# Token variance of a metaformer block: from VectorE to GpSimd, between two gate products, with new first and last steps

## What is computed

```python
x = x + attention(ln_c(x))            # windows of 8x8, 4 heads of 16, relative bias, projection
t = tokens(x)                         # 64 channels a token
n = (t - mean(t)) / sqrt(var(t) + 1e-5)
p = softmax(n @ router_w + router_b)  # 8 experts, the best two, their weights made to sum to 1
t = t + sum over the two of p_e * (n @ expert_w[e] + expert_b[e])
```

## Time and profile before

| | us |
|---|---|
| median of 3 runs | 1184.91 |
| lowest, highest | 1181.35, 1187.77 |
| the profiled execution | 1189.28 |
| its span, first to last instruction | 1187.5 |
| PE busy | 1053.8 (89%) |
| DVE busy | 891.9 (75%) |
| ACT busy | 745.1 (63%) |
| POOL busy | 429.3 (36%) |

### The profile page before, as it was taken

One profiled execution on the slowest core, in us unless ns is written; L12 is line 12 of the kernel. 1 busy time (PEld: TensorE's weight loads), 2 busy tenths in 40 slices (PEclk: granted clock), 3 DMA queues, 4 the chain that ended last, 5 costly groups with the idle time before them and its releaser, 6 DMA issues.

```text
span 1187.5 us, 39116 instructions
## 1 busy us (share of the span) xinstructions
PE 1053.8 (89%) x16838; PEld 602.3 (51%) x16838; DVE 891.9 (75%) x1441; ACT 745.1 (63%) x1217; POOL 429.3 (36%) x423
## 2 busy tenths in 40 slices
PE   5987899999899989999998988999998989988754
PEld 3654455555455555555555554555555545554311
DVE  4667777898787778988877776888887877678652
ACT  2777566766676677776676664767766666655400
POOL 1004244334424433344334333334442343335543
PEclk9999899999999999999999998999999999998877
DMA  5016476788776667887876667777776778647787
GB/s 183 2 38 155 98 162 165 177 187 192 185 165 162 162 169 172 186 196 182 198 166 142 160 160 170 180 173 175 178 175 152 182 179 198 140 100 170 189 182 176
DMA packets 49255, 192.48 MB, mean 162 GB/s; under 512 B 10558, under 2 KB 10814, under 8 KB 32572
## 3 DMA queue, kind: packets, MB, share of 16 engines
q1 hardware_dynamic: 49084, 189.98, 67.3%
HBM read 154.04 MB, written 18.87 MB: 146 GB/s over the span
## 4 chain that ended last, share of the span: by engine, by line
PE 77%; DMA 7%; issue 7%; DVE 5%; POOL 2%; ACT 1%; SPq 0%; POOLq 0%; ACTq 0%; DVEq 0%
PE bank L654 16%; PE bank L549 11%; PE bank L566 11%; PE bank L540 6%; PE bank L583 6%; DMA gz<-gates_dram 5%; PE bank L527 5%; PE bank L590 5%; PE bank L497 4%; PE bank L602 3%; PE bank L611 2%; PE bank L629 2%; PE bank L640 2%; PE bank L488 1%; PE bank L474 1%
## 5 line engine op out<-in xcount | busy, mean ns | idle before, releaser
L1480 POOL TENSOR_TENSOR gz<-gz,tt 128x1024 f32<-128x1024 f32 x96 | 240.5, 2506 | 134.0 <-DMA gz<-gates_dram 134.0
L654 PE MATMUL bank<-gz,wex 64*64 64x512 f32 x2048 | 262.1, 617 | 22.6 <-DVE gz L1682 17.2
L1076 ACT ACTIVATE pt<-bank 128x512 f32<-128x512 f32 x256 | 151.6, 592 | 140.2 <-PE bank L566 139.9
L1667 DVE TENSOR_TENSOR probs<-bank,mx 128x1024 f32<-128x1024 f32 x128 | 156.7, 1224 | 98.4 <-PE bank L566 95.3
L1682 DVE TENSOR_TENSOR gz<-gz,tt 128x1024 f32<-128x1024 f32 x160 | 201.4, 1277 | 26.4 <-DMA gz<-gates_dram 26.4
L1452 POOL TENSOR_TENSOR tt<-prj,xs 128x512 f32<-128x512 f32 x64 | 80.4, 1278 | 318.3 <-ACT prj L1093 318.3
L1660 DVE TENSOR_REDUCE mx<-bank 128x16 f32<-128x1024 f32 x128 | 156.1, 1220 | 36.0 <-PE bank L549 34.9
L566 PE MATMUL bank<-cst,probs 128*128 128x128 f32 x1024 | 167.6, 287 | 2.4 <-ACT pt L1076 1.6
L549 PE MATMUL bank<-km,qs 32*64 32x128 f32 x4096 | 146.8, 278 | 16.0 <-issue 16.0
L566 PEld LDWEIGHTS bank<-cst,probs 128*128 128x128 f32 x1024 | 113.1, 143 | 85.4 <-issue 72.0
L549 PEld LDWEIGHTS bank<-km,qs 32*64 32x64 f32 x4096 | 113.5, 133 | 65.1 <-issue 65.1
(11 more groups left out here) (110 smaller groups left out, 1429.2 us busy)
## 6 DMA issues: line engine op xcount, KB each, us to landing
gz<-gates_dram SPq DMA_DIRECT2D x256, 512.0 KB, 10.3
xs<-in_x SPq DMA_DIRECT2D x32, 512.0 KB, 9.0
tx<-tt SPq DMA_DIRECT2D x128, 128.0 KB, 2.9
out<-ob SPq DMA_DIRECT2D x128, 128.0 KB, 10.1
gz<-in_rel SPq DMA_DIRECT2D x1, 2048.0 KB, 8.1
gates_dram<-gt_rs SPq DMA_DIRECT2D x32, 64.0 KB
cst<-in_consts SPq DMA_DIRECT2D x1, 359.0 KB, 2.9
tt<-in_weights SPq DMA_DIRECT2D x4, 64.0 KB, 8.9
```

The lines of the kernel that those rows point to most:

```text
L654: last = mm(bank[64 * x:64 * x + 64, Y_BANK + a, :], wex[64 * a:64 * a + 64, e, :], gz[64 * a:64 * a + 64, s.pair(e)[1], e % 2, x * CH:(x ...
L1076: af(pt[g % 2][:, u % 2, :, :, :, :].rearrange("p j h x q -> p (j h x q)"), bank[:, PT_BANK, :], ACT.Copy).then_inc(pt_ready, 1)
L1480: tt_(gz[:, k, e % 2, :], gz[:, k, e % 2, :], tt[s.buf(4)][:, :], op=ALU.mult).then_inc(z_pool, 1)
L1667: tt_(probs[g % 2][:, :, :, :].rearrange("p h w (m k) -> p (h w m) k", k=N), two_banks(S_BANK).rearrange("p (c k) -> p c k", k=N), mx[g % ...
```

## The change

The three operations of token_statistics go from VectorE to GpSimd, with a semaphore of their own, moment. In the loop they stand between GpSimd's gated(c-6, 7) and gated(c-5, 1). VectorE's chain through top has two steps less. The warm-up and the drain have new orders on all five queues. The loop's orders on the other engines stay. The core of the diff; of the reordered lists only parts are shown:

```diff
+        moment = sem("moment")
-        TOP = 16
+        TOP = 14
...
 @@ SyncE, warm-up
             load_weights()
+            load_relative()
             load(strips[0])
             move_selection()
-            load_relative()
...
 @@ SyncE, drain
             spread_gates(strips[-5], 0)
             spread_gates(strips[-5], 1)
+            store(strips[-7])
+            swap_tokens(strips[-5])
             spread_gates(strips[-5], 2)
             spread_gates(strips[-5], 3)
...
+            write_gates(strips[-2])
             store(strips[-4])
-            swap_tokens(strips[-2])
-            write_gates(strips[-2])
             spread_gates(strips[-2], 0)
...
             write_gates(strips[-1])
-            store(strips[-3])
+            swap_tokens(strips[-2])
             spread_gates(strips[-1], 0)
             spread_gates(strips[-1], 1)
             spread_gates(strips[-1], 2)
             spread_gates(strips[-1], 3)
+            store(strips[-3])
...
 @@ GpSimd
+            def token_statistics(s):
+                pool.wait_ge(L_ready, s.count(2, 2))
+                wait(pool, lnr_done, s.count(1, 0))
+                tt_(mq[:, :, :, :], st_[:, :, 0:2, :], st_[:, :, 0:2, :], op=ALU.mult).then_inc(moment, 1)
+                pool.wait_ge(moment, s.count(2, 1))
+                tt_(vr[:, :].rearrange("p (c t a) -> p t c a", c=2, a=2), st_[:, :, 2:4, :], mq[:, :, :, :],
+                    op=ALU.subtract).then_inc(moment, 1)
+                pool.wait_ge(moment, s.count(2, 2))
+                nc.gpsimd.tensor_scalar(vr[:, :], vr[:, :], 0.0, 1e-5, ALU.max, ALU.add).then_inc(stat_ready, 1)
...
 @@ GpSimd, loop
                 gated(strips[c - 6], 7)
+                token_statistics(strips[c - 4])
                 gated(strips[c - 5], 1)
                 place_gates(strips[c - 4])
...
 @@ GpSimd, drain
             gated(strips[-5], 7)
+            place_gates(strips[-4])
             residual(strips[-3], 0)
             residual(strips[-3], 1)
-            place_gates(strips[-4])
...
             gated(strips[-3], 1)
-            gated(strips[-3], 4)
-            gated(strips[-3], 7)
             place_gates(strips[-2])
             residual(strips[-1], 0)
             residual(strips[-1], 1)
+            gated(strips[-3], 4)
+            gated(strips[-3], 7)
+            token_statistics(strips[-1])
             gated(strips[-2], 1)
             place_gates(strips[-1])
...
 @@ VectorE
-            def token_statistics(s):
-                dve.wait_ge(L_ready, s.count(2, 2))
-                top_step(s, 1, tt_(mq[:, :, :, :], st_[:, :, 0:2, :], st_[:, :, 0:2, :], op=ALU.mult))
-                top_step(s, 2, tt_(vr[:, :].rearrange("p (c t a) -> p t c a", c=2, a=2), st_[:, :, 2:4, :],
-                                   mq[:, :, :, :], op=ALU.subtract))
-                nc.vector.tensor_scalar(vr[:, :], vr[:, :], 0.0, 1e-5, ALU.max, ALU.add).then_inc(stat_ready, 1)
...
 @@ VectorE, warm-up
+            one_hot()
             norm_ready()
             variance(strips[0])
             guard_variance(strips[0])
             split_std(strips[0])
             scale_x(strips[0])
-            one_hot()
...
 @@ VectorE, loop
                 move_logits(strips[c - 4])
-                token_statistics(strips[c - 4])
                 normalise(strips[c - 3], 0)
                 gated(strips[c - 5], 0)
```

More of the change, by code:

```diff
@@ L398, in _ @@
             spread_gates(strips[-4], 2)
+            swap_tokens(strips[-4])
             spread_gates(strips[-4], 3)
             write_gates(strips[-3])
+            store(strips[-5])
             spread_gates(strips[-3], 0)
@@ L661, in _ @@
             channel_sums(strips[0])
+            bias_rows()
             spread_std(strips[0])
@@ L892, in _ @@
             denominators(strips[-3], 3)
-            transposes(strips[-2], 1)
+            transposes(strips[-2], 0)
+            experts(strips[-6], 4)
             experts(strips[-6], 5)
@@ L1132, in _ @@
             square_mean(strips[0])
+            square(strips[1])
             log_var(strips[0])
@@ L1138, in _ @@
             move_k(strips[0], 1)
-            square(strips[1])
             square_mean(strips[1])
@@ L1490, in _ @@
             residual(strips[1], 1)
+            token_statistics(strips[1])
             gated(strips[0], 1)
+            gated(strips[0], 4)
             place_gates(strips[1])
-            gated(strips[0], 4)
             residual(strips[2], 0)
@@ L1798, in _ @@
             shift(strips[1], 0)
+            scale_x(strips[2])
             normalise(strips[0], 2)
@@ L1802, in _ @@
             normalise(strips[0], 3)
-            scale_x(strips[2])
             row_max(strips[1], 2)
             shift(strips[1], 2)
-            normalise(strips[1], 0)
             row_max(strips[1], 3)
@@ L1817, in _ @@
             top_two(strips[0])
+            normalise(strips[1], 1)
             pick_two(strips[0])
+            split_std(strips[3])
+            gates(strips[0])
+            row_max(strips[2], 0)
             normalise(strips[1], 2)
-            row_max(strips[2], 0)
             shift(strips[2], 0)
-            gates(strips[0])
+            scale_x(strips[3])
             normalise(strips[1], 3)
@@ L1825, in _ @@
             shift(strips[2], 1)
-            split_std(strips[3])
             row_max(strips[2], 2)
             shift(strips[2], 2)
-            scale_x(strips[3])
             row_max(strips[2], 3)
-            normalise(strips[2], 0)
-            shift(strips[2], 3)
             variance(strips[4])
@@ L1835, in _ @@
             move_logits(strips[1])
-            token_statistics(strips[1])
+            shift(strips[2], 3)
+            normalise(strips[2], 0)
             logits(strips[1])
@@ L1842, in _ @@
             split_std(strips[4])
+            gated(strips[0], 0)
             gates(strips[1])
@@ L1955, in _ @@
             normalise(strips[-2], 0)
+            row_max(strips[-1], 0)
+            shift(strips[-1], 0)
             move_logits(strips[-3])
-            token_statistics(strips[-3])
+            gated(strips[-4], 0)
+            normalise(strips[-2], 1)
+            row_max(strips[-1], 1)
+            shift(strips[-1], 1)
+            normalise(strips[-2], 2)
             logits(strips[-3])
@@ L1961, in _ @@
             top_two(strips[-3])
-            normalise(strips[-2], 1)
-            row_max(strips[-1], 0)
-            shift(strips[-1], 0)
             pick_two(strips[-3])
-            gated(strips[-4], 0)
-            normalise(strips[-2], 2)
+            row_max(strips[-1], 2)
             gates(strips[-3])
-            row_max(strips[-1], 1)
-            shift(strips[-1], 1)
+            normalise(strips[-2], 3)
             gated(strips[-4], 2)
             gated(strips[-4], 3)
-            normalise(strips[-2], 3)
+            shift(strips[-1], 2)
             finish(strips[-5])
@@ L1977, in _ @@
             normalise(strips[-1], 0)
-            row_max(strips[-1], 2)
-            shift(strips[-1], 2)
             row_max(strips[-1], 3)
@@ L1982, in _ @@
             move_logits(strips[-2])
-            token_statistics(strips[-2])
-            gated(strips[-3], 0)
+            normalise(strips[-1], 1)
             logits(strips[-2])
-            normalise(strips[-1], 1)
             top_one(strips[-2])
@@ L2006, in _ @@
             pick_two(strips[-1])
+            finish(strips[-3])
+            gates(strips[-1])
             gated(strips[-2], 0)
-            gates(strips[-1])
             gated(strips[-2], 2)
```

506 lines of the change are left out of this document (250 added, 256 removed).

## The result

| | median us | runs | ratio to the kernel before, 95% interval |
|---|---|---|---|
| before, same chip | 1183.32 | 5 (1181.35 to 1187.77) | |
| after | 1165.29 | 5 (1159.65 to 1166.87) | 0.9837 [0.9808, 0.9867] |

The medians differ by 18 us, the ratio says 19; 8 were forecast. The time lies at the lower edge of the range. The profiled executions are 1189.28 us, longer than all five of before, and 1159.65, the shortest of after's.

The account below looks back on a forecast made before the run. It took TensorE to carry 77% of the chain, with VectorE's queue bounding the loop stretch it read and gates' transfers pacing the drain. Loop 0, drain -9, warm-up +1 gave -8: 1177 us, range 1165 to 1191.

Parts of the forecast that it names:

- The loop, "taken as 0": Loop, 25 passes: the block moves from the square to the logits, ending 4.25 against 4.22 us after st_; gain 0.
- The three small operations: Loop, GpSimd: square, difference and guard of the statistics cost 0.22+0.22+0.19 = 0.63 us, bounds 0.30 and 1.38.
- the gate product: Loop, GpSimd: gated(c-5, 1), queued behind the statistics, runs 2.36 us and ends near 4.1 us after st_.
- the logits: Loop, VectorE: L1734 waits for GpSimd's gate product and ends 4.25 us after st_, against 4.22 before.
- the first wait: Loop, TensorE before group 0's scores: the 0.95 us wait shrinks to under 0.5 us.
- the second: Loop, TensorE before group 1's scores: a wait appears, as large as the shrinkage before group 0's.
- The drain, -9: Drain: place_gates(-2) ends 9.7 us earlier, ahead of two strip -3 products; -9 us in sum, between -13 and 0.
- The warm-up, +1: Warm-up: table asked for before strip 0's input, first scores 2 us late, half given back; +1, between -4 and +5.
- The slower ones: Rivals on GpSimd's small operations: 0.46 us each gives 1196 us, chance 0.10; twice VectorE's time gives 1187, chance 0.08.
- The drain did gain: Answers a rival: the drain gains nothing because the gates' transfers, not their start, bound it; 1186 us, chance 0.25.
- GpSimd's small operations are not twice VectorE's: Answers a rival: GpSimd needs 0.35 us each, twice 0.18, +0.42 a pass, +10 us; 1187 us, chance 0.08.
- The cheap case: Rival, loop: GpSimd's small operations near 0.10 us and the variance out before VectorE's product; 1169 us, chance 0.12.

Follow-up runs that it names:

- loop_alone: Kernel before with the token statistics moved to GpSimd in the loop's 25 passes only, warm-up and drain orders as before; ratio 0.9892 to before.
- km_late: Kernel after with ScalarE's copy of the keys placed behind the next strip's log of variance and inverse_std; ratio 1.0004 to before.
- km_early: Kernel after with ScalarE's copy of the keys placed ahead of the tokens' log and root of variance in the loop; ratio 0.9747 to before.
- before_km_early: Kernel before with ScalarE's copy of the keys placed ahead of the tokens' log and root, statistics left on VectorE; ratio 0.981 to before.
- light_gates: Kernel before with each loop spread of the gates cut to 16 numbers a partition, so products read old gates; ratio 0.9721 to before.
- product_held: Kernel after with GpSimd's gate product held back until VectorE has made its picks, so the logits aren't blocked; ratio 0.9841 to before.

## Why the prediction was wrong, step by step

- **The loop, "taken as 0": the failed step.** Its parts hold. The three small operations cost 0.21, 0.22 unblocked and 0.27, 0.70 us against 0.63; the difference was blocked (1169 ns in the median); the gate product ended at T0+4.23 against 4.1; the logits at T0+4.37 against 4.25; the first wait shrank to 0.47 and the second opened with 0.61. The undisturbed pass is as long as before. What failed is the sentence "TensorE's first wait (0.95) shrinks and its second opens by as much; the earlier variance is hidden". It is hidden in a clean pass only. In about half of the passes the end is set by a third thing, TensorE's instruction fetch some 8 us later, and there the head start of the scores is passed on. In thirteen of before's fourteen stalled passes the fetch packet starts at T0+10.7 to 12.7; in the same passes of after the scores are 0.7 us earlier and the packet starts at T0+10.2 to 10.9, once at 9.2. The waits fall from 25.3 to 10.4 us. loop_alone measures the term at -13 us (-7 to -18). The remaining 5 us or so of the two profiles' 20 are about what the lower clock costs, in four passes before and one after; how often it falls differs between executions.
- **What could have been read before.** The earlier trace rows shows one nameless wait. The same view had 27.2 us more of them, at L583, L549, L488, L590 and L566, none in a place the change touches. "Nothing that the profile names" was not followed to its cause, and rows 5 and 6 are both strips without such a wait. The strip taken as representative was not.
- **Cause or company.** The start of the group-0 scores and the waits go together over km_late, before, after and km_early (5.4, 5.2, 4.5, 4.0 us; 25.4, 25.3, 10.4, 4.9 us) with the clean pass unchanged, and before_km_early shows it without any moved statistic. light_gates shows that the traffic is the other half. product_held marks the limit: with the same start of the scores as after (4.5) it has 25.5 us of waits: TensorE comes to its stop sooner (T0+11.3 in place of 12.2 in the tenth strip's pass). Why a head start of 0.7 us moves the packet by more than that in some passes (0.3 to 3.4 us in the thirteen) is argued, not shown: the packet is then asked for before more of the burst is queued.
- **The drain, -9: the mechanism right, the size 2 us off.** place_gates(-2) ended 8.4 us earlier against the loop, the last spread 7.4, the end 7.0. Most of the 2 us is the length of place_gates(-2), forecast at 3.6 us undisturbed. It took 5.35 (1088.07 to 1093.42), as long as in the kernel before (5.40), since two of its sums were blocked, one by each of VectorE's two products:

```profile
1088.77 2.61 DVE L1702 TENSOR_TENSOR gz<-gz,tt 128x1024 f32<-128x1024 f32 x2
1088.92 1.38 POOL L1466 TENSOR_TENSOR gp<-ga,gb 128x128 fp32r<-128x128 f32 x1
1090.26 1.43 POOL L1467 TENSOR_TENSOR gsum<-ga,gb 128x128 f32<-128x128 f32 x1
```

- **The warm-up, +1: about 0.** The first scores start 2.4 us later (33.18 against 30.78), 2 were forecast. The fourth strip's T0 lies at 173.6 against 175.7, but loop_alone, which leaves the warm-up as it was, has 173.2. A gain or loss below 2 us can't be told here.
- **The rivals.** The slower ones needed 0.40 us an operation; 0.23 was measured. The drain did gain. GpSimd's small operations are not twice VectorE's (0.23 against 0.18). The cheap case named a time near the result (1169) by a mechanism that didn't occur: the three end at T0+1.9, not before VectorE's product.
- **The sum.** Loop -13, drain -7, warm-up 0: -20, against -19 by the ratio.

## What to carry to other kernels

Add up all of an engine's nameless waits before choosing a strip to reason from, and look in the DMA queues for what lands as they end. Count the engine's records up to each such wait too: here all stood at the same place in a block of 256. A kernel that issues thousands of small matmuls also needs its instructions brought, here over the engines that carry its data. Where such a fetch sets the end of a pass, as here, work that starts earlier pays although the dependence behind it doesn't move (km_early), and a shorter dependence doesn't pay unless the fetch comes earlier too (product_held). The cheap trial is the order on one queue: here swapping the keys' copy with a statistic on ScalarE gave as much as the whole change.

## What was not expected of the hardware

- An instruction packet of 16 KB took 0.9 to 1.7 us on its DMA engine in the loops of before, after and light_gates, but TensorE stood up to 3.92 us (before) while transfers held the DMA engines at over 90%. With the gates' transfers cut, TensorE never waited for a packet in 24 passes.
- TensorE can stop for its instructions once in 256 records, always at the same place (193 or 194 past a multiple, 146 of 146 waits), and goes on 1.3 to 1.7 us after the packet's end (before and after).
- GpSimd's operation on 128x16 costs 0.21 to 0.27 us, half of the 0.46 of its 128x128 sum: the 0.46 is no fixed cost.
- Between two products of VectorE that stand back to back (1088.77, 2.61 us for both) GpSimd gets one instruction: its 128x128 sums of 0.45 us took 1.38 and 1.43, each held for one product. There a chain of short operations on GpSimd lost most of a product's length at each of two.
